# A graph attention layer on one core: softmax pieces, weighted tiles and a table load put in other places

## The reference

```python
h = relu(layernorm(x))
message = (h @ w_src + b_src)[src] + (h @ w_dst)[dst]          # 400000 x 128
rad_w = silu(silu(edge_attr @ w1 + b1) @ w2 + b2) @ w3 + b3
message = (message * edge_weight * rad_w) @ w_sep + b_sep      # 400000 x 256
alpha, value = split per head (8 heads, 16 + 16)
score = sum(smooth_leaky_relu(alpha) * alpha_dot)              # 400000 x 8
att = segment_softmax(score, dst)
out = x + segment_sum(value * att, dst) @ w_proj + b_proj
```

## Time and profile before

| | before |
|---|---|
| time, median of 3 runs | 5095.57 us (5094.09 to 5096.37) |
| time of the profiled execution | 5094.63 us |
| its span | 5092.7 us |
| PE busy | 4832.5 us, 95% |
| PEld busy | 3449.1 us, 68% |
| DVE busy | 3848.3 us, 76% |
| ACT busy | 2626.1 us, 52% |
| POOL busy | 3618.4 us, 71% |
| mean granted TensorE clock | 0.973 |

### The profile page before, as it was taken

The page is one execution under the profiler, slowest core; times in us unless marked ns, Lnnn a source line. Parts: engine busy times, 40 slices in busy tenths (PEclk is TensorE's granted clock), DMA queues, the critical chain, the costliest instruction groups (busy, mean ns, idle before and its releaser), DMA issues. The chain is left out here.

```text
span 5092.7 us, 92871 instructions
## 1 busy us (share of the span) xinstructions
PE 4832.5 (95%) x28995; PEld 3449.1 (68%) x28995; DVE 3848.3 (76%) x6981; ACT 2626.1 (52%) x3939; POOL 3618.4 (71%) x3491
## 2 busy tenths in 40 slices
PE   3599999999999999999999999999999999999975
PEld 2456777777776777777677777777777777777764
DVE  6547777777777777777777777777777777777777
ACT  2455555555555555555555555555555555555511
POOL 2377777777777777777777777777777777777716
PEclk9799999999999999999999999999999999999975
DMA  6666666666666666666666666766666666666625
GB/s 188 191 202 200 211 200 212 204 206 207 202 211 202 211 202 206 206 202 211 202 209 205 205 208 199 213 203 207 205 206 208 201 209 205 207 206 206 207 64 157
DMA packets 889681, 1019.24 MB, mean 200 GB/s; under 512 B 161780, under 2 KB 778008, under 8 KB 888863
## 3 DMA queue, kind: packets, MB, share of 16 engines
q1 hardware_dynamic: 758843, 774.32, 47.3%
q0 software_dynamic: 108784, 223.44, 17.6%
q10 hardware_dynamic: 21556, 15.50, 1.2%
HBM read 863.59 MB, written 152.34 MB: 199 GB/s over the span
## 5 line engine op out<-in xcount | busy, mean ns | idle before, releaser
L1056 POOL DMA_INDIRECT gath<-msg_src,idx x3328 | 3475.5, 1044 | 1176.5 <-issue 1030.8
L1245 ACT ACTIVATE sil<-a_ps,ba 128x512 f32<-128x512 f32 x832 | 571.7, 687 | 1648.1 <-PE a_ps L1367 1580.7
L1375 PEld LDWEIGHTS v_ps<-wv,msgT 128*128 128x128 f32 x6656 | 835.5, 191 | 526.2 <-issue 526.2
L1305 PEld LDWEIGHTS rad_ps<-wval,hot 128*128 128x128 f32 x6656 | 911.5, 194 | 79.0 <-DVE wval L1147 35.6
L1305 PE MATMUL rad_ps<-wval,hot 128*128 128x136 f32 x6656 | 929.3, 284 | 32.5 <-DVE wval L1147 31.3
L1375 PE MATMUL v_ps<-wv,msgT 128*128 128x128 f32 x6656 | 924.1, 282 | 0.0
L1367 PE MATMUL a_ps<-msgT,wa 128*128 128x512 f32 x1664 | 890.7, 617 | 30.9 <-DVE msgT L1178 30.9
L1178 DVE TENSOR_TENSOR msgT<-xT_ps,rads 128x512 f32<-128x512 f32 x832 | 572.4, 688 | 354.1 <-PE xT_ps L1348 307.9
L1197 DVE SCALAR_TENSOR_TENSOR sil<-a_ps,sil 128x512 f32<-128x512 f32 x832 | 567.4, 682 | 354.2 <-ACT sil L1245 351.6
L1294 PE MATMUL xT_ps<-hotT,win 128*128 128x256 f32 x3328 | 730.4, 341 | 0.0
L1230 ACT ACTIVATE vals<-v_ps 128x512 f32<-128x512 f32 x832 | 493.2, 593 | 340.4 <-PE v_ps L1375 319.0
(11 more groups left out here) (234 smaller groups left out, 4147.9 us busy)
## 6 DMA issues: line engine op xcount, KB each, us to landing
rows_bc<-edge_rows SPq DMA_DIRECT2D x416, 768.0 KB
win<-msg_dst SPq DMA_DIRECT2D x1664, 128.0 KB
sums<-run SPq DMA_DIRECT2D x416, 272.0 KB
attr<-in_edge_attr_t SPq DMA_DIRECT2D x1664, 32.0 KB
gath<-msg_src,idx POOLq DMA_INDIRECT x3328
msg_dst<-dst_parts SPq DMA_DIRECT2D x98, 128.0 KB, 2.2
pen_g<-pen_rows SPq DMA_DIRECT2D x208, 32.1 KB
mask_g<-mask_rows SPq DMA_DIRECT2D x208, 32.0 KB
```

The source lines that it names most:

```text
L1056: pool.indirect_dma_start(gath[:, u, s], None, msg_src, bass.IndirectOffsetOnAxis(ap=idx[:, j // 8, at:at + 1], axis=0)).then_inc(s_gath[u ...
L1245: act.activation(sil[:, j % 8], a_ps[:, :], ACT.Silu, bias=ba[:, :]).then_inc(s_sil, 1)
L1305: last = pe.matmul(rad_ps[:, j % 2, AW * i:AW * (i + 1)], lhsT=hot[:, j % 4, s], rhs=wval[:, j % 4, s].rearrange("p h k -> p (h k)"), star ...
L1375: last = pe.matmul(v_ps[:, s * P:(s + 1) * P], lhsT=msgT[:, q, s * P:(s + 1) * P], rhs=wv[:, :], start=True, stop=True)
```

## The change

Four things move.

1. On DVE the softmax pieces of the odd steps go to even steps: `shifted` from step 1 to step 0, the second `ends` and the maximum of both scans from step 5 to step 4, and the scan L1102 from step 9 to step 8. In an even step a piece stands between `accumulate` and the correction of `sil`; in an odd step it stood behind the latter.
2. `weigh` handles one tile per call and is called twice in an odd step: ahead of `accumulate` and behind it, where one call handled two tiles behind it.
3. In step 14, `factor` is read behind `mark` and no longer ahead of it.
4. Behind the exponentials of step 11, ACT applies SiLU to a column of 128 numbers that nobody reads (`spare`), so that the SiLU set is loaded there and not ahead of the `sil` of step 12.

```diff
--- before.py
+++ after.py
@@ -885,6 +885,7 @@
             h2 = tb("h2", [P, 2 * CE])
             apart = tb("apart", [P, 4, CE])
             row_below = tb("row_below", [P, 1])
+            spare = tb("spare", [P, 1])
             rads = tb("rads", [P, 4, TE])
             msgT = tb("msgT", [P, 2, TE])
             sil = tb("sil", [P, 8, TE])
@@ -1062,7 +1063,7 @@
                 def soft(n, j):
 
                     k = KS * n
-                    if j == 1:
+                    if j == 0:
                         dve.wait_ge(s_sc, 4 * n + 4)
                         dve.wait_ge(s_pm, 160 * n + 160)
                         need(dve, s_wp, n)
@@ -1074,7 +1075,6 @@
                         dve.tensor_tensor_scan(bwd[:, :][:, ::-1], pen[:, 1:TE + 1][:, ::-1], shifted[:, :][:, ::-1], -BIG, ALU.add, ALU.max).then_inc(s_soft, 1)
                         dve.wait_ge(s_soft, k + 2)
                         dve.tensor_scalar(ends[:, 0:G], sel[:, :], fwd[:, TE - 1:TE], None, ALU.mult).then_inc(s_soft, 1)
-                    elif j == 5:
                         dve.wait_ge(s_soft, k + 4)
                         dve.tensor_scalar(ends[:, G:2 * G], sel[:, :], bwd[:, 0:1], None, ALU.mult).then_inc(s_soft, 1)
                         dve.wait_ge(s_soft, k + 5)
@@ -1097,7 +1097,6 @@
                         dve.wait_ge(s_soft, k + 12)
                         dve.tensor_reduce(carry_in[:, :], carried[:, :, :], mybir.AxisListType.X, ALU.add).then_inc(s_soft, 1)
                         dve.tensor_copy(carry[:, 0:1], carry[:, G:G + 1]).then_inc(s_soft, 1)
-                    elif j == 9:
                         dve.wait_ge(s_soft, k + 14)
                         dve.tensor_tensor_scan(bwd[:, :], pen[:, 0:TE], fwd[:, :], carry_in[:, 0:1], ALU.add, ALU.max).then_inc(s_soft, 1)
                     elif j == 10:
@@ -1142,11 +1141,10 @@
                         if j == 0:
                             dve.wait_ge(s_wT, g + 1)
                     slot = G * (g % 2) + j
-                    for n in range(2):
-                        at = 32 * ((j + n) % 4) + H * (j // 4)
-                        last = dve.tensor_tensor(wval[:, u + n], vals[:, slot + n],
-                                                 wT[:, :, at:at + H].unsqueeze(3).broadcast_to((P, SUB, H, HV)), ALU.mult)
-                    last.then_inc(s_wv, 1)
+                    at = 32 * (j % 4) + H * (j // 4)
+                    product = dve.tensor_tensor(wval[:, u], vals[:, slot], wT[:, :, at:at + H].unsqueeze(3).broadcast_to((P, SUB, H, HV)), ALU.mult)
+                    if j % 2:
+                        product.then_inc(s_wv, 1)
 
                 def accumulate(g, j):
                     a = G * g + j
@@ -1176,27 +1174,27 @@
                         if j % 2 == 0:
                             dve.wait_ge(s_rads, t // 2 + 1)
                         dve.tensor_tensor(msgT[:, j % 2], xT_ps[:, :], rads[:, j % 4], ALU.mult).then_inc(s_msg, 1)
-                    if group(g - 1) and j == 14:
-                        soft(g - 1, j)
                     if j % 2 == 0:
                         if there(t + 2 - LAG):
                             mark(*later(g, j, 2 - LAG))
+                        if group(g - 1) and j == 14:
+                            soft(g - 1, j)
                         if there(t - LAG):
                             accumulate(*later(g, j, -LAG))
                         if group(g - 1) and j != 14:
                             soft(g - 1, j)
                     else:
+                        if there(t + 1 - LAG):
+                            weigh(*later(g, j, 1 - LAG))
                         if there(t - LAG):
                             accumulate(*later(g, j, -LAG))
-                        if there(t + 1 - LAG):
-                            weigh(*later(g, j, 1 - LAG))
+                        if there(t + 2 - LAG):
+                            weigh(*later(g, j, 2 - LAG))
                         if there(t + 1):
                             scale_rad(*later(g, j, 1))
                     if there(t):
                         dve.wait_ge(s_sil, t + 1)
                         dve.scalar_tensor_tensor(sil[:, j % 8], a_ps[:, :], 0.25, sil[:, j % 8], ALU.mult, ALU.add).then_inc(s_al, 1)
-                    if j % 2 and group(g - 1):
-                        soft(g - 1, j)
                 dve.memset(vals[:, :, :, :, AH], 1.0)
                 dve.memset(run[:, R - 1, 1], 0.0)
                 dve.memset(carry[:, :], -BIG).then_inc(s_clear, 1)
@@ -1250,6 +1248,7 @@
                         act.wait_ge(s_soft, KS * n + 17)
                         act.activation(shifted[:, :], shifted[:, :], ACT.Exp)
                         act.activation(drop[:, :], drop[:, :], ACT.Exp).then_inc(s_exp, 1)
+                        act.activation(spare[:, :], row_below[:, :], ACT.Silu)
                     if j % 2 == 0 and there(t + 2):
                         measure(*later(g, j, 2))
                 act.activation(row_below[:, :], row_number[:, :], ACT.Copy, scale=-1.0).then_inc(s_apart, 1)
```

## The result

The changed kernel takes 5047.98 us (median of 4 runs, 5044.98 to 5048.61) where the kernel before, in the same session, takes 5094.92 (4 runs, 5094.09 to 5096.37). The ratio is 0.9904, with an interval of 0.9891 to 0.9918: faster by 46.9 us. The forecast was 5060 in a range of 5050 to 5081: the direction is right, and the gain is 12 us larger than the sum of 34.9 and lies outside the range.

The account below looks back on a forecast made before the run. PE's own work was taken to set the pace, so only its waits could be won back: 25.5 (scan) + 2.1 (group 1) + 7.3 (drain) = 34.9 us off 5094.6 gives 5059.7, called 5060; range 5050 to 5081.

Parts of the forecast that it names:

- The scan: DVE, step 9 to step 8: step 10 takes 5.03 us instead of 5.54, 50 x 0.51 = 25.5 us gained.
- `shifted`: DVE, step 1 to step 0: goes into a wait of 0.7 us for `sil`, costed at nothing.
- The pieces of step 5: DVE, two pieces of 0.87 us moved to step 4: nothing lost there and nothing gained in step 5.
- what makes `sil` late is covered twice: DVE, even steps: a wait for `sil`, then the 1.25 us the next odd step's `msgT` waits, absorb moved work; cost nothing.
- One `wval` ahead of `run`: DVE, 400 odd steps: `run` could start 1.26 us after `msgT`, aggregate ready at 1.36, 0.10 to spare; taken as 0.
- Rival B: `wval` delays `run` by 0.02 to 0.06 us in each odd step: 8 to 24 us lost, 5068 to 5084; chance 0.14.
- PE goes on exactly when `run` is done: Odd steps: PE's weight loading is held 400 times, 322.8 us, by the second `run` ahead of `radial`.
- The table load: ACT, end of step 11: `vals` ends about 2092.56, PE starts 2092.62; taken as 0, or 5 us with semaphore delay.
- Rival D: Start of step 12: early table load holds `vals` and PE's turning of the weights; slower, for example 5125; chance 0.08.
- Group 1: Nothing is aggregated there, so late `msgT` is less covered: 1.1 us at step 10, half each at steps 2 and 6; 2.1 gained.
- The drain: First `wval` leaves the chain: 0.67 us a pair, 10 pairs, 6.7 us; with the smaller items 7.3 us gained.

Follow-up runs that it names:

- c1: The kernel before with only the scan of step 9 moved to step 8; 5062.12 us, ratio 0.9933 to the kernel before.
- e5: The changed kernel with both `wval` ahead of `run` in the odd steps, on a chip with stalls; 6100.11 us, ratio 0.9915 to the kernel before.
- e9: The changed kernel with two dummy DVE products ahead of `msgT` in each of steps 2 and 10; 5076.07 us, ratio 0.9964 to the kernel before.
- c3: The changed kernel without the small SiLU, so the table loads ahead of `sil` in step 12 again; 5042.06 us, ratio 0.9893 to the kernel before.
- c4: The changed kernel with both `wval` behind `run` in the odd steps, as before; 5056.68 us, ratio 0.9921 to the kernel before.

## Why the prediction came out 12 us short

**The scan, 25.5 us: the mis-sized term.** The mechanism was right, and the scan alone (c1) gives 32.5 us. The failing step is "PE's step 10 should take the 5.03 us of step 2". Step 2 had a piece of its own in front of `msgT` and lost 0.15 us itself, so that the unhindered step is 4.88 and the term 50 x 0.66 = 33. I looked for stalls in the list of waits, found none of step 2 there, and took its length as clean.

**`shifted`, costed at nothing.** It costs nothing in step 0, as said; but in step 1 it had cost 0.15 a group, and this gain is missing from the sum: 7.5 us. The two errors have one root, and together they are 50 x 0.30 = 15 us. The other errors are smaller: the drain gave 3.8 us more than its term, the table load took 4, and some 3 are left over below. So the 12 us by which the sum is short are mainly these 15.

**The pieces of step 5**, nothing: step 6 goes from 5.242 to 5.230, 0.6 us in all. In steps 0, 4 and 8, which took the work over, nothing is lost (6.073 and 6.074, 6.072 and 6.074, 6.617 before and 6.614 after in step 8). That what makes `sil` late is covered twice was right.

**One `wval` ahead of `run`**, nothing in the steps: right. Spare time was put at 0.10 and is 0.14, shown from both sides (e5 and e9). Rival B, a small loss here, is out. `wval` starts 0.61 us after `msgT`, which is 0.69 long. The rule of the Trainium skill (VectorE: DVE Perf Modes, "The DRAIN you can't avoid") that the prediction weighed, and which would have added 12 us, is therefore not the one for this place; the same section adds that "A next op that is not held starts earlier", and with that the trace agrees. The prediction left this sentence out. My sentence that PE goes on exactly when `run` is done holds for lateness (e5: 0.50 us a step); an earlier release could gain at most about 0.05 us a step.

**The table load**, 0 with a bound of 5: it costs 0.06 us in step 12 (6.62 to 6.68; c1 and c3, which have no small SiLU, stay at 6.62), 3 us over the groups. The missing term is the 0.11 us between the end of `vals` and the weight load behind it, as the mean of groups 3 to 49; the prediction had `vals` end 0.06 us ahead of PE's start and called that punctual. In e9, whose late step 11 lets `vals` end 0.19 us earlier in step 12, the small SiLU stands and step 12 takes 6.62. In group 1 it costs 1.0, for there PE does wait:

```profile
398.13 0.63 PE L1330 MATMUL v_ps<-ident,shifted 128*128 128x128 f32 x4 [0.99 <-ACT vals L1228]
```

These 4 us are within the bound. Rival D fell: the activation behind the load starts 1.29 us after it, as the earlier trace rows had it, and the load starts 0.21 us after the start of `drop`, which is 0.19 long. The drain of 1.38 us that the Trainium skill (ScalarE: Activation LUTs, "What ACT_TABLE_LOAD costs") counts with a switch shows nowhere. What the load left behind, an earlier `sil` of DVE in step 12, brings nothing, as said (c3 has it late again and loses nothing in any step).

**Group 1**, 2.1 us: steps 2, 6 and 10 took 5.08, 5.24 and 5.61 and now take 4.64, 4.57 and 4.64, which is 2.08. Step 12 gives 1.02 of it back.

**The drain**, 7.3 us and measured 11.1. That the first `wval` leaves the chain is right: PE's wait for it falls by 0.64 a pair, as forecast. PE in two pairs before, and in three after:

```profile
4933.36 3.63 PE L1305 MATMUL rad_ps<-wval,hot 128*128 128x136 f32 x16 [2.11 <-DVE wval L1147]
4939.10 3.27 PE L1305 MATMUL rad_ps<-wval,hot 128*128 128x136 f32 x16 [2.11 <-DVE wval L1147]
```
```profile
4892.85 2.12 PE L1304 MATMUL rad_ps<-wval,hot 128*128 128x136 f32 x16 [1.47 <-DVE wval L1145]
4896.81 2.75 PE L1304 MATMUL rad_ps<-wval,hot 128*128 128x136 f32 x16 [1.84 <-DVE wval L1145]
4901.03 3.99 PE L1304 MATMUL rad_ps<-wval,hot 128*128 128x136 f32 x16 [1.47 <-DVE wval L1145]
```

But the same 16 products take 2.12 and 2.75 us in some pairs, where before they took 3.3 to 3.6. The windows over six pairs, of before, of after, and of c4, which has both `wval` behind `run`:

```profile
4927.20:4961.70 34.50, 21.79 (x96) 20.10 (x96) 22.96 (x42) 0.00 (x0) 0.00 (x0) 0.60 0.16 49
```
```profile
4887.30:4914.70 27.40, 17.74 (x97) 16.06 (x97) 22.82 (x43) 0.00 (x0) 0.00 (x0) 0.75 0.20 62
```
```profile
4893.00:4927.00 34.00, 21.34 (x96) 19.65 (x95) 21.70 (x41) 0.00 (x0) 0.00 (x0) 0.60 0.16 50
```

The granted clock is 0.60 before and in c4 and 0.75 after: between 1.2 and 2.4 GHz, four fifths of the stretch at the lower level against half of it. A pair takes 4.6 us instead of 5.75, 1.2 less where 0.67 was forecast; the rest is the clock, with which PE's own work in six pairs fell from 21.8 to 17.7 us. The split brings both: c4 shows it, and from the last tile's `xT_ps` to the last `run` the eleven traces of kernels with a `wval` ahead of `run` take 80 to 86 us, the seven without 94 to 96, whatever the chip; that the clock rose because PE waits less between its products is argued, not shown. Pairs of the drain's beginning gained less, so that the error of the term is 3.8 us.

The sum as it should have been: 33 + 7.5 + 2.1 + 11.1 - 4 = 49.7, against 46.9. Of the 2.8 left, 1.7 are the later start of the edge stage and 0.4 the last stage, which the change does not touch; the start lies between 254.9 and 257.4 us in the six kernels of the table above.

**Open.** On the chips with the stalls only kernels with a `wval` ahead of `run` are faster, by 1%, more than their drains explain. `rads` then has 0.60 us of slack in every odd step, which might take in a part of the stalls; no run tells whether it does.

The fastest version is the changed kernel without the small SiLU: 5042.06 us, 0.9893 of the kernel before.

## What to carry to other kernels

Before one step is priced as the difference to another, look whether that other is itself free of stalls: compare the length of its products, and whether its weight loads start ahead of them, with a step of the same products whose operand is in time. A list of waits counts idle time of an engine, and that is not what a late operand costs: here PE's named 20 us and PEld's 30.5 for step 10, neither named step 2, and the cost was 41 (50 x 0.66 and 50 x 0.15). And a wait that the list does name, in full view for 322 us, can be worth far less: about 20 us by estimate. To learn it by a run, every product that waits must be freed, not the first alone.

## What the runs showed of the hardware

- A wait that stands ahead of a product in PE's queue holds its weight load too, even where the operand waited for is not the weights: the load of `wa` started 0.05 us after the end of a late `msgT`. In time it would have run 0.11 us ahead of its product, while the product before still ran. The price of being late was lateness less 0.31 us over five values from 0.25 to 1.00, where nothing else stands between the aggregate and `a_ps`. Whether a load ahead of the wait would save it was not tried.
- In the drain, a chain of short bursts, the wait of PE became 0.64 us shorter a pair, the granted clock was 0.75 instead of 0.60, and a pair took 1.2 us less, nearly twice the wait.
- DVE starts an instruction 0.60 to 0.63 us after one of 0.68 to 0.71 us (`msgT`, `wval` and `run` in step 11 of e9): an instruction of this size costs 0.1 us less than its row when one follows that does not wait for it. The second `run`, which waits for the first, started 0.04 us after its end (2018.58 + 0.35 to 2018.97).
- The same kernel took 5094 to 5095 us on some chips and 6156 to 6198 on three others. The changed kernel had in the same 900 us a clock of 0.95 against 1.00, 169 against 208 GB/s of transfers and 114 against 0.2 us of idle PE, on the chip of session 2 and on that of the result. A delay of 0.50 us in 400 steps cost only 10 us there.
